# Issuing the two DMAs of the row maxima from ScalarE's queue in an attention and feed-forward kernel, with a new plan

## The reference

```python
x = layernorm(x + attention(x, Wq, Wk, Wv, Wo))   # x: 8 x 512 x 512, float32
x = layernorm(x + ffn(x, weight, bias))

def attention(x, Wq, Wk, Wv, Wo):    # 16 query heads, 4 key/value heads, head size 32
    q, k, v = x @ Wq, x @ Wk, x @ Wv          # heads split off, k and v repeated 4 times
    attn = softmax(q k^T / sqrt(32))          # over 512 keys, for each head and query
    return (attn v) @ Wo

def ffn(x, weight, bias):            # int8 quantization, one scale per row
    w_scale = clip(max|weight|, 1e-8) / 127;  w_q = round(weight / w_scale)
    x_scale = max(max|x| / 127, 1e-12);       x_q = round(x / x_scale)
    return (x_q w_q^T) * x_scale * w_scale + bias
```

## Time and profile before

| what | value |
|---|---|
| median of 3 runs | 786.63 us (784.62 to 788.5) |
| profiled execution | 787.02 us, span 785.2 us |
| granted TensorE clock, mean | 0.985 |
| PE busy | 735.6 us (94%) |
| DVE busy | 615.2 us (78%) |
| POOL busy | 596.8 us (76%) |
| ACT busy | 477.5 us (61%) |
| DMA queue of SP | 55152 packets, 61.91 MB |

### The profile page before, as it was taken

One profiled execution on the slowest core, in us unless ns is written; L12 is line 12 of the kernel. 1 busy time (PEld: TensorE's weight loads), 2 busy tenths in 40 slices (PEclk: granted clock), 3 DMA queues, 4 the chain that ended last, 5 costly groups with the idle time before them and its releaser, 6 DMA issues.

```text
span 785.2 us, 12326 instructions
## 1 busy us (share of the span) xinstructions
PE 735.6 (94%) x3700; PEld 433.8 (55%) x3700; DVE 615.2 (78%) x1090; ACT 477.5 (61%) x872; POOL 596.8 (76%) x705
## 2 busy tenths in 40 slices
PE   8789989899899999999999999999999999999993
PEld 6455545566366654566446663666545664454451
DVE  3797888668987788886888789878888868888546
ACT  3165556556765576656666566656756666666735
POOL 4258858676997689885987779975998759898935
PEclk9799999999999999999999999999999999999997
DMA  7632223133231342223322332413422233022121
GB/s 213 175 95 55 56 58 96 52 91 101 67 111 46 101 100 91 69 72 91 95 80 71 95 101 63 122 41 94 108 84 68 76 93 102 28 56 67 51 47 54
DMA packets 56386, 65.57 MB, mean 84 GB/s; under 512 B 25665, under 2 KB 27713, under 8 KB 56321
## 3 DMA queue, kind: packets, MB, share of 16 engines
q1 hardware_dynamic: 55152, 61.91, 29.5%
q0 software_dynamic: 1168, 2.89, 1.5%
HBM read 20.71 MB, written 8.39 MB: 37 GB/s over the span
## 4 chain that ended last, share of the span: by engine, by line
PE 45%; POOL 16%; issue 15%; SPq 10%; ACT 4%; DVE 4%; DMA 3%; POOLq 3%; DVEq 0%; ACTq 0%
POOL prob_sum L1080 14%; PE front_bank L341 9%; SPq L312 9%; PE st_bank L416 8%; PE s_bank L385 7%; PE o_bank L433 7%; PE tail_bank L341 6%; PE z_bank L459 3%; POOLq L1089 2%; DVE row_max L865 2%; ACT probs L695 1%; PE front_bank L348 1%; PE tail_bank L529 1%; DMA xq_sb<-round_sb 1%; POOL x_tok L1098 1%
## 5 line engine op out<-in xcount | busy, mean ns | idle before, releaser
L865 DVE TENSOR_REDUCE row_max<-s_bank 128x1 f32<-128x512 f32 x496 | 329.1, 682 | 81.2 <-PE s_bank L385 78.4
L695 ACT ACTIVATE probs<-st_bank 128x512 f32<-128x512 f32 x512 | 290.4, 594 | 133.1 <-PE st_bank L416 114.5
L1080 POOL TENSOR_TENSOR prob_sum<-prob_sum,probs 128x512 f32<-128x512 f32 x248 | 310.6, 1285 | 8.1 <-ACT probs L695 8.1
L416 PE MATMUL st_bank<-q_stack,k_stack 98*128 98x512 f32 x512 | 224.6, 441 | 14.6 <-ACT probs L695 11.1
L385 PE MATMUL s_bank<-k_stack,q_stack 96*128 96x512 f32 x496 | 203.4, 412 | 8.3 <-DVE row_max L865 7.1
L1080 POOL TENSOR_TENSOR prob_sum<-probs 128x512 f32<-128x512 f32 x128 | 161.3, 1284 | 46.0 <-PE z_bank L459 23.9
L416 PEld LDWEIGHTS st_bank<-q_stack,k_stack 98*128 98x128 f32 x512 | 96.1, 188 | 104.8 <-ACT probs L695 55.0
L433 PE MATMUL o_bank<-probs,v_tok 128*32 128x512 f32 x1024 | 123.3, 598 | 0.1
L385 PEld LDWEIGHTS s_bank<-k_stack,q_stack 96*128 96x128 f32 x496 | 94.2, 190 | 40.2 <-DVE row_max L865 22.5
L1085 POOL TENSOR_TENSOR rs<-mv,small 128x1 f32<-128x1 f32 x64 | 12.2, 190 | 82.1 <-DVE mv L915 81.5
L433 PEld LDWEIGHTS o_bank<-probs,v_tok 128*32 128x32 f32 x1024 | 26.7, 109 | 59.4 <-issue 52.5
(11 more groups left out here) (199 smaller groups left out, 992.8 us busy)
## 6 DMA issues: line engine op xcount, KB each, us to landing
q_stack<-q_parts SPq DMA_DIRECT2D x348, 64.0 KB, 2.0
x_tok<-in_L_attn_x SPq DMA_DIRECT2D x36, 256.0 KB, 3.0
y_sb<-in_L_attn_x SPq DMA_DIRECT2D x28, 256.0 KB, 2.8
out<-z_sb SPq DMA_DIRECT2D x28, 256.0 KB, 2.1
k_stack<-k_parts SPq DMA_DIRECT2D x84, 64.0 KB, 2.0
probs<-in_L_attn_Wq SPq DMA_DIRECT2D x1, 1024.0 KB, 7.6
prob_sum<-in_L_attn_Wo POOLq DMA_DIRECT2D x4, 256.0 KB, 4.3
q_stack<-neg_max SPq DMA_DIRECT2D x64, 8.0 KB, 1.8
```

The lines of the kernel that those rows point to most:

```text
L416: nc.tensor.matmul(st_bank[:, j % 2, :], k_stack[0:STACK_M, p, j, kt * P:(kt + 1) * P], q_stack[0:STACK_M, i, j, :], start=True, stop=True ...
L695: nc.scalar.activation(probs[:, kt, j, :], st_bank[:, j % 2, :], ACT.Exp, scale=SCALE).then_inc(exp_done, 1)
L865: nc.vector.tensor_reduce(row_max[:, i % 2, j * QT + qt:j * QT + qt + 1], s_bank[:, qt % 2, :], AX_X, ALU.max).then_inc(max_done, 1)
L1080: nc.gpsimd.tensor_tensor(prob_sum[:, j, :], first, probs[:, kt, j, :], ALU.add).then_inc(sum_done, 1)
```

## The change

`stack_max` goes from SyncE's program to ScalarE's, with its wait on `ml_done`. It gets an entry of its own in the three plans, `stack_max_act`, and stands behind `max_hi` of the same unit and ahead of the copies of the front. The two DMAs, their sizes and their semaphores stay. All other entries of the plans are set anew; most stay or move by one or two units. The diff, of the plans what the text speaks of:

```diff
 MIDDLE = dict(
...
-    front_pe={Q3: (0, 1, 3, 4), 0: (5,), 1: (10,), 2: (13,), 3: (16,), K: (18, 22), Q0: (23, 24, 25, 27), V: (29, 30), VT: (33,), Q1: (36, 37), Q2: (44, 45)},
-    front_act={Q3: 3, 0: 5, 1: 10, 2: 13, 3: 16, K: 22, Q0: 27, V: 29, VT: 32, Q1: 38, Q2: 45},
-    front_dve={Q3: 4, 0: 6, 1: 11, 2: 15, 3: 16, K: 22, Q0: 27, Q1: 39, Q2: 45},
+    front_pe={Q3: (0, 1, 3, 4), 0: (5,), 1: (10,), 2: (13,), 3: (16,), K: (19, 22), Q0: (23, 24, 25, 27), V: (29,), VT: (34,), Q1: (36, 38), Q2: (43, 45)},
+    front_act={Q3: 3, 0: 5, 1: 10, 2: 15, 3: 16, K: 22, Q0: 26, V: 32, VT: 34, Q1: 38, Q2: 45},
+    front_dve={Q3: 3, 0: 6, 1: 11, 2: 14, 3: 16, K: 22, Q0: 27, Q1: 39, Q2: 46},
...
-    max_lo_dve=(11, 26, 45, 59),
-    o_hi_act=(10, 29, 46, 57),
...
-    wo_pe=((9, 11, 14), (19, 20, 21, 22), (31, 34), (39, 40, 42)),
-    load_sp=(5, 17, 27, 39),
...
-    rstd1_pool=(23, 27, 38, 45),
+    max_lo_dve=(11, 26, 43, 57),
+    stack_max_act=(13, 27, 46, 61),
+    o_hi_act=(11, 29, 47, 60),
...
+    wo_pe=((9, 11, 14), (19, 20, 21, 22), (33, 34), (39, 40, 42)),
+    load_sp=(6, 17, 25, 37),
...
+    rstd1_pool=(22, 28, 37, 45),
...
-    round_act=(21, 31, 39, 47),
-    unround_act=(22, 31, 43, 52),
-    turn_sp=(21, 29, 42, 49),
-    bias_pool=(26, 38, 44, 55),
-    load_x_sp=(1, 2, 3, 7),
-    ffn_pe=(27, 36, 48, 56),
...
+    round_act=(22, 31, 43, 47),
+    unround_act=(22, 33, 43, 52),
+    turn_sp=(19, 29, 44, 49),
+    bias_pool=(25, 39, 45, 55),
+    load_x_sp=(0, 1, 2, 13),
+    ffn_pe=(28, 36, 48, 56),
...
-    norm2_act=(35, 40, 55, 62))
+    norm2_act=(36, 40, 55, 63))
 FIRST = dict(
...
-    front_act={Q3: 4, 0: 7, 1: 10, 2: 12, 3: 14, K: 21, Q0: 25, V: 29, VT: 34, Q1: 41, Q2: 50},
...
+    front_act={Q3: 6, 0: 7, 1: 9, 2: 12, 3: 13, K: 21, Q0: 25, V: 30, VT: 33, Q1: 42, Q2: 50},
...
-    max_lo_dve=(12, 25, 42, 57),
...
-    load_x_sp=(1, 2, 2, 6))
...
+    max_lo_dve=(13, 25, 42, 56),
+    stack_max_act=(13, 26, 43, 58),
...
+    load_x_sp=(0, 1, 4, 6))
 LAST = dict(
...
-    max_lo_dve=(13, 27, 43, 59),
...
+    max_lo_dve=(12, 27, 44, 61),
+    stack_max_act=(14, 28, 44, 62),
...
-    turn_sp=(26, 30, 46, 57),
...
-    load_x_sp=(28, 35, 53, 59),
-    ffn_pe=(28, 38, 53, 59),
...
+    turn_sp=(23, 31, 46, 52),
...
+    load_x_sp=(29, 37, 57, 61),
+    ffn_pe=(28, 38, 52, 60),
...
 def plan_of(front, tail):
...
                 act.wait_ge(mt_done, b * GROUPS + i + 1)
                 nc.scalar.mul(neg_max[:, 0, :].bitcast(F32R), o_bank[0:NKV * QT, 0:P], -1.0).then_inc(mh_done, 1)
+            def stack_max(b, i):
+                act.wait_ge(ml_done, b * GROUPS + i + 1)
+                for n in range(2):
+                    act.dma_start(q_stack[STACK + n:STACK + n + 1, i, :, :].bitcast(F32), neg_max[:, n, :]).then_inc(m_stacked[i], 16)
+
             def o_split_hi(b, i):
                 n = b * GROUPS + i
                 act.wait_ge(norm_done, n + 1)
...
                         i = plan["max_hi_act"].index(u) + 1
                         if i < GROUPS or front:
                             max_hi(b + i // GROUPS, i % GROUPS)
+                    if u in plan["stack_max_act"]:
+                        i = plan["stack_max_act"].index(u) + 1
+                        if i < GROUPS or front:
+                            stack_max(b + i // GROUPS, i % GROUPS)
                     for f, unit in plan["front_act"].items():
                         if u == unit and (front or f == Q3):
                             front_in_turn(b if f == Q3 else b + 1, p if f == Q3 else 1 - p, f)
...
             first_front(Q1)
             wq_part(3)
             max_hi(0, 0)
+            stack_max(0, 0)
             first_front(Q2)
             segment(0, 0, front=True, tail=False)
             for b in range(1, B - 1):
...
                     wait(sp, st_done, (b - 1) * UNITS + (i + 1) * QT * NKV)
                     stack_heads(sp, range(NKV), q_stack[:, i, :, :], (hi, hi, lo), q_stacked[i])
-            def stack_max(b, i):
-                sp.wait_ge(ml_done, b * GROUPS + i + 1)
-                for n in range(2):
-                    sp.dma_start(q_stack[STACK + n:STACK + n + 1, i, :, :].bitcast(F32), neg_max[:, n, :]).then_inc(m_stacked[i], 16)
-
             def load_residual(b, t):
                 if b == 0 and t == 0:
                     sp.wait_ge(w_bcast, 1)
...
             def segment(b, p, front, tail):
                 plan = plan_of(front, tail)
                 for u in range(UNITS):
-                    if u in plan["max_lo_dve"]:
-                        i = plan["max_lo_dve"].index(u) + 1
-                        if i < GROUPS or front:
-                            stack_max(b + i // GROUPS, i % GROUPS)
                     for o in range(KC):
                         if not tail and u == WEIGHT_LOAD_SP[o]:
                             load_weight(o)
...
             for j in range(NKV):
                 first_stack_k(sp, j)
             stack_front(0, 0, Q1, first_parts[Q1])
-            stack_max(0, 0)
             segment(0, 0, front=True, tail=False)
             for b in range(1, B - 1):
                 segment(b, b % 2, front=True, tail=True)
```

More of the change, by code:

```diff
@@ L77 @@
-    res2_dve=(30, 36, 52, 60),
-    stats2_dve=(33, 38, 52, 61),
+    max_lo_dve=(11, 26, 43, 57),
+    stack_max_act=(13, 27, 46, 61),
+    o_hi_act=(11, 29, 47, 60),
+    o_lo_dve=(12, 29, 47, 62),
+    wo_pe=((9, 11, 14), (19, 20, 21, 22), (33, 34), (39, 40, 42)),
+    load_sp=(6, 17, 25, 37),
+    res1_dve=(15, 22, 34, 43),
+    stats1_dve=(17, 23, 35, 44),
+    rstd1_pool=(22, 28, 37, 45),
+    norm1_act=(18, 27, 38, 47),
+    maxx_dve=(19, 27, 39, 47),
+    round_act=(22, 31, 43, 47),
+    unround_act=(22, 33, 43, 52),
@@ L79 @@
+    turn_sp=(19, 29, 44, 49),
+    bias_pool=(25, 39, 45, 55),
+    load_x_sp=(0, 1, 2, 13),
+    ffn_pe=(28, 36, 48, 56),
+    rescale_dve=(31, 36, 49, 58),
+    res2_dve=(31, 37, 52, 60),
+    stats2_dve=(34, 37, 52, 61),
     rstd2_pool=(36, 40, 56, 63),
-    norm2_act=(35, 40, 55, 62))
+    norm2_act=(36, 40, 55, 63))
 FIRST = dict(
-    front_pe={Q3: (5,), 0: (8,), 1: (10,), 2: (12,), 3: (13,), K: (16, 19, 21, 22), Q0: (23, 24), V: (28, 29), VT: (31,), Q1: (36, 38, 41), Q2: (44, 45, 50)},
@@ L83 @@
[L83 to L84 removed]
+    front_pe={Q3: (5,), 0: (8,), 1: (10,), 2: (11,), 3: (14,), K: (16, 19, 21, 22), Q0: (23, 24), V: (28, 30), VT: (32,), Q1: (36, 38, 41, 42), Q2: (44, 50)},
+    front_act={Q3: 6, 0: 7, 1: 9, 2: 12, 3: 13, K: 21, Q0: 25, V: 30, VT: 33, Q1: 42, Q2: 50},
+    front_dve={Q3: 6, 0: 8, 1: 9, 2: 12, 3: 14, K: 21, Q0: 26, Q1: 42, Q2: 51},
@@ L85 @@
     sums_pe=(11, 23, 35, 53),
[L86 to L89, removed]
+    inv_act=(16, 23, 37, 54),
+    correct_dve=(3, 22, 38, 55),
+    scale_dve=(20, 23, 40, 55),
+    norm_dve=(2, 28, 43, 62),
     max_pe=(9, 25, 42, 57),
-    max_hi_act=(10, 25, 42, 56),
-    max_lo_dve=(12, 25, 42, 57),
-    o_hi_act=(14, 30, 47, 63),
-    o_lo_dve=(4, 30, 51, 62),
-    load_x_sp=(1, 2, 2, 6))
+    max_hi_act=(10, 25, 42, 57),
@@ L96 @@
+    max_lo_dve=(13, 25, 42, 56),
+    stack_max_act=(13, 26, 43, 58),
+    o_hi_act=(12, 28, 46, 63),
+    o_lo_dve=(5, 30, 49, 63),
+    load_x_sp=(0, 1, 4, 6))
 LAST = dict(
-    front_pe={Q3: (0, 1, 3, 5, 9)},
-    front_act={Q3: 9},
-    front_dve={Q3: 13},
+    front_pe={Q3: (1, 2, 3, 4, 5)},
+    front_act={Q3: 8},
+    front_dve={Q3: 12},
     sums_pe=(6, 22, 37, 55),
[L101 to L104, removed]
@@ L120 @@
-    bias_pool=(21, 36, 52, 61),
-    load_x_sp=(28, 35, 53, 59),
-    ffn_pe=(28, 38, 53, 59),
-    rescale_dve=(28, 38, 49, 60),
+    inv_act=(6, 23, 37, 55),
+    correct_dve=(7, 23, 38, 53),
+    scale_dve=(7, 23, 40, 56),
+    norm_dve=(8, 23, 40, 56),
+    max_pe=(10, 28, 42, 63),
+    max_hi_act=(11, 26, 43, 63),
+    max_lo_dve=(12, 27, 44, 61),
+    stack_max_act=(14, 28, 44, 62),
+    o_hi_act=(9, 30, 42, 59),
+    o_lo_dve=(11, 35, 42, 61),
+    wo_pe=((10, 11, 13, 14), (20, 23, 25), (31, 34, 35, 36), (40, 44)),
@@ L124 @@
+    load_sp=(4, 13, 28, 42),
+    res1_dve=(15, 25, 35, 43),
+    stats1_dve=(15, 27, 36, 44),
+    rstd1_pool=(18, 30, 40, 50),
+    norm1_act=(18, 30, 38, 53),
+    maxx_dve=(20, 29, 40, 46),
+    round_act=(21, 31, 43, 54),
+    unround_act=(25, 34, 45, 58),
+    turn_sp=(23, 31, 46, 52),
+    bias_pool=(26, 40, 54, 60),
+    load_x_sp=(29, 37, 57, 61),
+    ffn_pe=(28, 38, 52, 60),
+    rescale_dve=(28, 38, 49, 61),
     res2_dve=(29, 38, 49, 61),
-    stats2_dve=(29, 42, 49, 61),
-    rstd2_pool=(32, 47, 57, 62),
@@ L127 @@
-    norm2_act=(35, 46, 59, 63))
+    stats2_dve=(29, 42, 49, 63),
+    rstd2_pool=(38, 46, 58, 63),
+    norm2_act=(36, 45, 59, 63))
 def plan_of(front, tail):
```

21 lines of the change are left out of this document (2 added, 19 removed).

## The result

The changed kernel takes 793.13 us in the median of 6 runs (792.21 to 795.92), the kernel before 787.79 us in 6 runs on the same chip (784.62 to 790.87). The ratio is 1.0064 [1.0034, 1.0095]: slower by 0.6%. The forecast, 786.0 us and no change that can be told, was wrong; the 793.13 us lie in its range.

A forecast was written before the change was run, and what follows sets the result against it. Bounds taken: TensorE from unit 5 to 39, GpSimd's adds from unit 39 to the next unit 5. Terms -2.5 (SyncE) - 0.5 (first batch) + 2.4 (ScalarE) = -0.6 us: 786.0 us median; range 779.5 to 794.

The forecast's parts named there:

- All pieces placed anew: Pieces moved one to three units inside the two stretches of a middle batch; claimed 0 us.
- a first stretch no longer 53.9 us: Sign of wrong: units 5 to 39 off 53.9 us would mean a replaced piece opened a wait priced at nothing.
- GpSimd as full as before from unit 39 to unit 5: Sign of right: GpSimd stays as busy from unit 39 to the next batch's unit 5, 35.51 of 36.77 us before.
- The first batch: Wait for the maxima at unit 16, 1.55 us: 0.5 us saved; replaced pieces there 0, +-1.5 us.
- Relief of SyncE: DMAs leaving SyncE's queue shorten the long middle batches: -2.5 us, of 3.4 us at full relief.
- unit 48: Weight load waiting for the maxima's landing: near 0.5 us saved in each of two batches.
- ScalarE's price: DMAs issued on ScalarE, 0.589 us each: +2.4 us, 0.4 us in each of 6 batches.
- unit 46: Pair behind an exp on ScalarE: of 1.18 us 0.3 hidden, 0.9 passed on, 0.4 left after GpSimd's cover.
- unit 27: Pair on ScalarE covered by the 2.37 us freed when the copy of V moves: cost 0.
- The landing in group 3: Landing of the pair issued at unit 46: no earlier in batch 4, earlier in the long batches.
- The second, 794 us: Slower: ScalarE's pair and SyncE's twelve DMAs take turns, each issue two turns of 0.589 us; +8 us, chance 0.24.
- The first rival: Faster, 780.5 us: issues run beside the exps, ScalarE adds 0, SyncE's relief is whole; -6.5 us, chance 0.28.

The follow-up runs named there:

- newplan_sp: The changed kernel's new plans, but with the DMAs of the maxima issued from SyncE's queue as before; ratio 1.0069 to the kernel before.
- before_hole: The kernel before, DMAs on SyncE, with three middle-plan entries changed: Q2's first half 43, third max_lo 43, last residual 43; ratio 1.0057.
- oldplan_act: The kernel before with its old plans, but the DMAs of the maxima issued from ScalarE at units 13, 27, 46, 61 in the middle; ratio 1.0016.
- after_g3_sp: The changed kernel with group 3's pair of DMAs (unit 46) of the middle batches issued by SyncE; ratio 1.0062 to the kernel before.
- after_repair: The changed kernel with three middle-plan entries set back: Q2's first half 44, third max_lo 45, last residual 42; 792.08 us, ratio 1.0040.
- after_q2_44: The changed kernel with only the first half of Q2 set back from unit 43 to 44; 792.04 us, ratio 1.0035 to the kernel before.

## Why the prediction was wrong

**The step that failed** is "All pieces placed anew ... moving pieces inside them gives nothing: 0". It costed the new plan from the busy share of two stretches, and the second stretch was the argument against it: GpSimd was full there, 35.51 of 36.77 us, so a late input of GpSimd's could open a gap there with nothing to make it good. I looked for work that crossed the border of the stretches and did not follow the three moved entries inside: half a projection a unit earlier on TensorE, then a row maximum 0.50 us late, then `mv` 0.57 us late, then 0.95 us of nothing on the engine that sets the end of the stretch. Of the 0.95 us, 0.58 us were left in the length of the stretch. newplan_sp and before_hole show it. The sign that I named for a badly placed piece, a first stretch no longer 53.9 us, looked at the wrong stretch (53.84 us); another, GpSimd as full as before from unit 39 to unit 5, looked at the right one. The direct price in TensorE's waits is 2.6 us in the changed kernel, 3.2 in before_hole and 5.2 in newplan_sp; the times, 0.57% and 0.69% for before_hole and newplan_sp, or 4.5 and 5.4 us, lie near or above that. An estimate brings them to one clock, by a straight line through each kernel's runs, time against mean granted clock (only 6 to 12 runs each beside the kernel before, so good to about 1 us): at 0.980 the kernel before takes 789.6 us, before_hole 792.6 us, the changed kernel 793.3 us, newplan_sp 794.8 us. The hole's 3.0 us then agree with its 3.2 us of waiting, and the rest of its 4.5 us came with a lower clock (0.979 in the mean of its runs, 0.983 in those of before beside them).

**The first batch** was forecast 0.5 us shorter, within 1.5 us. It came out 2.67 us longer in the profiled execution, and 1.2 to 1.8 us shorter than the 86.59 us of before in the three other profiles with the same instructions there. So the forecast of this term is not refuted; the profiled execution was the odd one of four. What I had left out is still in the sentence that I did write, that SyncE no longer stops at `ml_done`: a load of 256 KB then moves forward in SyncE's queue, ahead of the maxima. I credited what was behind the maxima in the queue and not what would now be ahead of them; that it costs time is not shown.

**The move itself was near in size in both terms, and in part by luck.** Relief of SyncE: -2.5 us forecast; the wait for the transposed tile falls by 2.2 to 2.6 us where the plan is the old one (3.0 to 0.8, 0.4 and 0.6 us), by 1.3 us in the changed kernel. I had put only 1.5 us there and 1.0 us at unit 48, where TensorE now stands 2.28 us in three batches of the changed kernel, before 1.83 us in two. ScalarE's price: +2.4 us forecast, all in the middle batches; TensorE's wait for the exps rises by 2.5 to 3.2 us with the old plan (11.1 us to 13.6, 13.7 and 14.3 us), but only 1.2 to 1.8 us of that are in the middle batches; in the changed kernel it rises by 1.4 us. Each issue was forecast at 0.589 us and took 0.592 us in the median. The place was wrong in part: at unit 46 the pair passed on 0.31 us, not 0.9, since the first issue runs beside the copy of Q2 and the second beside the exp, as ScalarE's rows in batch 4 of the changed kernel show, which answer to the earlier trace rows:

```profile
471.85 0.58 ACT L660 CAST q_parts<-front_bank 128x512 fp32r<-128x512 f32 x1 [0.97 <-PE front_bank L344]
472.04 0.52 ACTq L717 DMA_DIRECT2D q_stack<-neg_max  x1
472.33 0.60 ACT L698 ACTIVATE probs<-st_bank 128x512 f32<-128x512 f32 x1
472.59 0.61 ACTq L717 DMA_DIRECT2D q_stack<-neg_max  x1
473.25 0.60 ACT L698 ACTIVATE probs<-st_bank 128x512 f32<-128x512 f32 x1 [0.31 <-issue]
```

And unit 27, costed at nothing because the copy of V was to move, cost 0.8 to 1.0 us a batch where the copy of Q0 stayed behind the pair (oldplan_act). In the changed kernel that copy had moved to unit 26, which the diff showed and I had not weighed: of all pieces placed anew it is the one that the move needed.

**The landing in group 3** comes no earlier in batch 4, as forecast: the weight load of unit 48 waits 0.86 us, had 0.96 us. In the long batches, where I had forecast that it would, it did not do so in the changed kernel either (the 2.28 us above). Batch 4:

```profile
474.50 0.19 PEld L419 LDWEIGHTS st_bank<-q_stack,k_stack 98*128 98x128 f32 x1 [0.86 <-DMA q_stack<-neg_max]
```

**The rivals.** The second, 794 us, had the time and not the mechanism: no issue took two turns as a rule, and after_g3_sp does not mend it. The Trainium skill's rule behind it ("Perfetto Trace Analysis", section "DMA Instruction — HWDGE (DVE, Sync)", one issuing engine at a time) is not seen at that size: 23 issues beside SyncE's were longer by 0.001 and 0.004 us in the median. The first rival's free ScalarE time (32.4 us a batch by the earlier trace rows; I wrote 31) did not hide the pairs.

**What stays open.** after_repair is still at 1.0040. TensorE waits in it 1.7 us more for the exps than in the kernel before and 0.9 us more for the maxima (3.4 against 2.5 us), but 0.6 us less for the sums, 1.5 us less for the tile and 1.6 us less for row maxima (5.5 against 7.1 us): 1.1 us less in all. What is more is TensorE's busy time, 743.1 against 735.6 us for the same 3700 instructions, so the granted clock (0.979 against 0.985 in the two profiled executions). At a clock of 0.980 the line through its runs gives 791.2 us, 1.6 us above the kernel before.

Whether the moved pieces bring the falls of the clock is not settled, but the traces lean that way at one place. In the five kernels with the hole, the granted clock fell to 1.2 GHz within 0.4 us of the start of the sums of unit 54 in 5 of 30 middle batches, each time at a wait of 0.95 to 1.05 us before them; in the eight others (among them after_q2_44 with its smaller gap), in none of 48. One of the five, in newplan_sp (TensorE, then the window with its columns as in the earlier trace rows):

```profile
483.45 1.93 PE L462 MATMUL z_bank<-prob_sum,ones 128*32 128x512 f32 x8 [1.04 <-POOL prob_sum L1083]
```

```profile
483.40:486.80 3.40, 3.35 (x14) 0.94 (x18) 1.43 (x4) 1.27 (x3) 3.12 (x6) 0.50 0.53 65
```

after_repair has none there, so what lowers its clock stays open.

## What to carry to other kernels

When a change comes with a new schedule, price the schedule first: follow every moved piece to the next instruction of the engine that is full, since here a late input of half a microsecond was paid in whole, and a busy share near 100% is a reason to look and not a reason to write 0. When a wait is taken out of a queue, list what moves forward past it as well as what was held back by it. Before a single profile is believed on such a place, look at others with the same instructions. Run the schedule and the edit apart: here the edit alone changed nothing that can be told, the schedule alone cost as much as both, and the old schedule with one copy set ahead of the new work and one load held back gave the lowest time.
